# Gate products, residual and second normalisation on other engines in a fused Mamba and expert layer

## The chip, the core and the metric

The kernel runs on one core of a Trainium2 chip. The metric is device time in microseconds of one execution, median of several; inputs and outputs are float32 throughout.

## What is computed

For x of 4 batches of 2048 positions and 256 channels, with a modulation (sa, ca, ga, sb, cb, gb) computed from a small vector per batch:

```
h = layernorm(x) * (1 + ca) + sa
xs, res = split(h @ in_proj.T)
u = silu(conv4(xs) + conv_b)                    # 512 inner channels
dt, B, C = split(u @ x_proj.T)
delta = softplus(dt @ dt_proj.T + dt_b)
h_t = exp(delta*A) * h_{t-1} + (delta*u) * B    # 16 states per channel
y = sum_n(h_t * C) * silu(res)
x = x + ga * (y @ out_proj.T)
h = layernorm(x) * (1 + cb) + sb
x = x + gb * (shared expert(h) + best of 7 routed experts(h), by their gates)
```

An expert is `(silu(h @ w1b) * (h @ w1a)) @ w2`. The gate of the shared expert is a softmax over one logit.

## The kernel before

Two stages follow one another. The first, `fused_program`, takes all 8192 positions in 16 chunks of 512 (`NCHUNK`, `T`); it does everything up to the shared expert and writes rows and logits to memory. The second routes each position to one expert and runs the experts, tile by tile; the change does not touch it.

In a chunk the 512 channels times 16 states are cut into 16 sets of 32 channels (`NSET`); a set fills 128 partitions with 4 groups of states, so it has four scans of 128 x 512. For each set s of chunk c:

- SyncE spreads delta over the partitions by DMA (`spread_delta`), and ScalarE makes dA = exp(A * delta) into one of three PSUM banks (`exps`, L703, `ABANK`), so that it can be three scans ahead.
- The input delta*u*B of the set is written into one of eight state buffers `hs` (`RING`): for ten sets by VectorE, out of `u_ps` where TensorE spread delta*u (L816), for six sets (2, 5, 7, 10, 13, 15) by GpSimd, out of `u_rep`, spread by DMA (L986). GpSimd works in `states_in` only when the sum of the states that were in the buffer is made (`y_ready`).
- VectorE runs the four scans (L829). ScalarE saves the last column (L728), after which GpSimd multiplies the states by C (`weigh_states`, L993). TensorE adds up 16 states of four sets at a time: groups SUM 0 to 3 (L507), which VectorE gates with silu(res) (L838).

Everything else is woven between the scans. The work of a chunk is staggered: its front part (T, XS, CV, RS, XP, DT, DB: transposed normalised x, the projections, convolution, delta) runs one chunk ahead, its back part (OP: output projection; T2, RB, GL, B, A, Y: second normalised rows turned, written out, logits, shared expert) one chunk late. Four tables written out by hand say in which set each engine does what, with an offset that says for which chunk: `plan` for TensorE, `evict` for ScalarE (after which of the set's four exponentials), `vector` for VectorE (after which scan), `gps` for GpSimd, and `transfers` the order of SyncE's queue. Each engine and queue runs strictly in the order of its table.

TensorE's groups go to three banks: what ScalarE reads shares two, in the order of the plan; what VectorE reads (`VECTOR`, L225: SUM, OP, DB, A, Y) shares the third. A group waits until the group before it in its bank is read.

What the change and the prediction name:

- `weigh_u` (L800, at L804): delta*u for half a chunk, 128 x 1024, both inputs in SBUF, on VectorE; DU in the tables.
- `gate_norm` (L854 to L862): exp/sum for the shared gate, on VectorE: reciprocal, product, reciprocal, product, of 128 x 4.
- `residual` (L840, L845): x plus the output projection out of PSUM, on VectorE.
- `layernorm2` (L781 to L790): statistics of the second normalisation on VectorE; `rsqrt`, `rsqrt2` (L953 to L969): the inverse roots of both normalisations on GpSimd, by a power; `normalize`, `normalize2` (L650, L656) on ScalarE.
- `exp_table` (L647): loads ScalarE's table set that has both exponential and logarithm. SU is silu of u, SR and SS silu of res and of the shared expert's gate half, ET the loading of that set, E and L exponential and logarithm of the softplus.

## Time and profile before

| | |
|---|---|
| time, median of 3 runs | 2807.65 us (2804.6 to 2808.03) |
| the profiled execution | 2804.95 us, span 2803.1 us |
| busy: TensorE, VectorE, ScalarE, GpSimd | 2235.7, 2189.8, 1434.2, 1891.8 us |
| scan stage | from 76 us to 2226 us, first product with u_ps to last scan |
| expert stage | from 2300 us on |
| ScalarE table loads in four chunks | 28 (L648 8, L721 8, L633, L637, L641 4 each) |

A busy time counts an engine's instructions, without its waits. In a row of a group "busy, mean ns of one" is followed by the idle time of the engine just before those instructions and by what ended it. A float32 product of TensorE gives two records.

### The profile page before, as it was taken

The numbers are of one execution on the slowest core, as the hardware profiler recorded it, in microseconds if no ns is written. First come the engines' busy times: TensorE is split into PE (matmuls) and PEld (weight loads), VectorE is DVE, ScalarE is ACT, GpSimd is POOL, SyncE is SP. The second block draws the span as 40 slices with busy tenths as digits, with TensorE's granted clock in tenths as the row PEclk, the third lists the DMA queues.
The fourth block names the chain that finished last, engine by engine and source line by source line (L and its number), as shares of the span: only waits on it lengthen the run. The fifth ranks groups of instructions, "written<-read, shape, count | busy, mean of one in ns | idle before, by whom it ended". The sixth has DMA issues, their size and how long they took to land. (4 is left out here: it accounts for less than half of the span.)

```text
span 2803.1 us, 31106 instructions
## 1 busy us (share of the span) xinstructions
PE 2235.7 (80%) x7664; PEld 1062.5 (38%) x7665; DVE 2189.8 (78%) x2130; ACT 1434.2 (51%) x2391; POOL 1891.8 (67%) x800
## 2 busy tenths in 40 slices
PE   7759787978787788878786969697975656999997
PEld 3214332433333333434242424242432334666564
DVE  2799999998999999999999999999999625222222
ACT  4566474747474747474656565656554313222221
POOL 0788777777786878787868687777878602555553
PEclk9778999888889998989898989898986877999999
DMA  4433141313231323232323232323232124222221
GB/s 127 145 96 92 52 98 49 97 53 99 61 92 54 92 56 89 61 91 72 80 68 79 70 77 77 81 75 82 66 80 64 35 62 152 88 83 86 84 87 48
DMA packets 149399, 224.38 MB, mean 80 GB/s; under 512 B 48227, under 2 KB 85617, under 8 KB 145138
## 3 DMA queue, kind: packets, MB, share of 16 engines
q1 hardware_dynamic: 136914, 186.63, 25.3%
q0 software_dynamic: 12320, 35.93, 4.3%
q8 instruction: 57, 0.93, 0.2%
q14 instruction: 108, 0.88, 0.1%
HBM read 99.48 MB, written 31.47 MB: 47 GB/s over the span
## 5 line engine op out<-in xcount | busy, mean ns | idle before, releaser
L993 POOL TENSOR_TENSOR hs<-hs,c_rep 128x2048 f32<-128x2048 f32 x256 | 1170.2, 4585 | 258.1 <-ACT state L728 257.6
L721 ACT ACTIVATE dA<-d_rep,a 128x512 f32<-128x512 f32 x1024 | 689.9, 686 | 591.9 <-DVE hs L829 583.9
L829 DVE TENSOR_TENSOR_SCAN hs<-dA,state,hs 128x512 f32<-128x512 f32 x768 | 930.4, 1262 | 34.3 <-ACT dA L721 30.4
L986 POOL TENSOR_TENSOR hs<-u_rep,b_rep 128x2048 f32<-128x2048 f32 x96 | 444.9, 4634 | 181.1 <-DMA u_rep<-us 173.2
L478 PE MATMUL bank<-n,w1s 128*128 128x512 f32 x512 | 278.3, 676 | 142.9 <-DVE xpad L852 128.7
L816 DVE TENSOR_TENSOR hs<-u_ps,b_rep 128x2048 f32<-128x2048 f32 x160 | 361.4, 2276 | 9.8 <-PE u_ps L497 5.0
L507 PE MATMUL bank<-hs,spread 128*32 128x512 f32 x2048 | 297.0, 732 | 54.7 <-POOL hs L993 50.0
L436 PE MATMUL bank<-xin,w_in 128*128 128x512 f32 x512 | 268.9, 663 | 58.1 <-ACT xdbl L603 48.1
L829 DVE TENSOR_TENSOR_SCAN hs<-dA,hs 128x512 f32<-128x512 f32 x256 | 294.4, 1202 | 21.4 <-ACT dA L721 20.5
L1365 DVE TENSOR_TENSOR hid<-z,sg 128x512 f32<-128x512 f32 x70 | 48.4, 692 | 297.9 <-ACT sg L1343 297.9
L1283 PE MATMUL z<-w1r,hT 128*128 x560 | 260.8, 609 | 3.0 <-issue 2.0
L440 PE MATMUL bank<-xpad,w_conv 128*128 128x512 f32 x512 | 226.3, 595 | 0.0
L478 PEld LDWEIGHTS bank<-n,w1s 128*128 128x128 f32 x512 | 98.7, 209 | 297.6 <-DVE xpad L852 166.0
L497 PE MATMUL u_ps<-us,spread 32*128 32x512 f32 x320 | 189.5, 683 | 0.0
L455 PE MATMUL bank<-w_out,res 128*128 128x256 f32 x512 | 138.4, 432 | 49.3 <-DVE res L838 47.7
L436 PEld LDWEIGHTS bank<-xin,w_in 128*128 128x128 f32 x512 | 101.2, 206 | 201.5 <-issue 130.5
L507 PEld LDWEIGHTS bank<-hs,spread 128*32 128x32 f32 x2048 | 71.9, 131 | 273.8 <-issue 236.9
L1250 POOL DMA_INDIRECT out<-outr,cur x70 | 70.8, 1011 | 142.8 <-DVE outr L1358 140.4
L447 PE MATMUL bank<-xdbl,w_dt 65*128 65x512 f32 x256 | 137.1, 650 | 34.5 <-ACT n L614 14.7
L1283 PEld LDWEIGHTS z<-w1r,hT 128*128 128x128 f32 x560 | 101.4, 191 | 120.8 <-issue 120.6
L1343 ACT ACTIVATE sg<-z 128x512 f32<-128x512 f32 x70 | 41.8, 597 | 201.8 <-PE z L1283 196.2
L455 PEld LDWEIGHTS bank<-w_out,res 128*128 128x128 f32 x512 | 110.5, 218 | 87.7 <-issue 52.4
(174 smaller groups left out, 2718.9 us busy)
## 6 DMA issues: line engine op xcount, KB each, us to landing
d_rep<-delta SPq DMA_DIRECT2D x1024, 64.0 KB, 2.0
u_rep<-us SPq DMA_DIRECT2D x384, 64.0 KB, 2.0
b_rep<-bc_rows SPq DMA_DIRECT2D x64, 256.0 KB, 4.4
c_rep<-bc_rows SPq DMA_DIRECT2D x64, 256.0 KB, 7.4
xin<-in_x SPq DMA_DIRECT2D x16, 512.0 KB, 7.6
xres<-in_x SPq DMA_DIRECT2D x16, 512.0 KB, 3.6
token_rows<-xpad SPq DMA_DIRECT2D x32, 256.0 KB, 2.9
token_rows<-xres SPq DMA_DIRECT2D x16, 512.0 KB, 2.9
```

Of the source, the lines that this page charges most:

```text
L436: last = nc.tensor.matmul(ps_[:, :], t["w_in"][:, k, col:col + P], hT[:, k, :], start=(k == 0), stop=(k == KD - 1))
L440: last = nc.tensor.matmul(ps_[:, :], t["w_conv"][:, j, k, :], xpad[:, j, k:k + T], start=(k == 0), stop=(k == KCONV - 1))
L455: last = nc.tensor.matmul(ps_[:, h * D:(h + 1) * D], res[:, (par + off) % 2, k, tt * P:(tt + 1) * P], t["w_out"][:, k, :], start=(k == 0), ...
L478: last = nc.tensor.matmul(ps_[:, :], t["w1s"][:, k, col:col + P], h2T[:, k, :], start=(k == 0), stop=(k == KD - 1))
L497: nc.tensor.matmul(u_ps[:, i % 2, :], t["spread"][DS * q:DS * q + DS].rearrange("p f d -> p (f d)"), us[DS * q:DS * q + DS, par, j, :], st ...
L507: last = nc.tensor.matmul(ps_[DS * q:DS * q + DS, :], t["gather"], hs[:, (SPC * j + q) % RING, n, :], start=(n == 0), stop=(n == NG - 1), ...
L721: nc.scalar.activation(dA[:, u % ABANK, :], d_rep[:, q, :], ACT.Exp, scale=t["a"][:, u:u + 1]).then_inc(da_ready, 1)
L816: nc.vector.tensor_tensor(hs[:, s % RING], u_ps[:, i % 2, :].unsqueeze(1).to_broadcast([P, NG, T]), b_rep[:, par, :].rearrange("p (g t) -> ...
L829: nc.vector.tensor_tensor_scan(hs[:, s % RING, g, :], dA[:, u % ABANK, :], hs[:, s % RING, g, :], state[:, u:u + 1] if m else 0.0, ALU.mul ...
L986: nc.gpsimd.tensor_tensor(hs[:, s % RING], u_rep[:, i % UBUF, :].unsqueeze(1).to_broadcast([P, NG, T]), b_rep[:, par, :].rearrange("p (g t ...
L993: nc.gpsimd.tensor_tensor(hs[:, s % RING, :, :], hs[:, s % RING, :, :], c_rep[:, par, :].rearrange("p (g t) -> p g t", g=NG), ALU.mult).th ...
L1283: last = nc.tensor.matmul(z[:, q % 2, half, :], hT[:, q % 2, i, :], t["w1r"][:, e, i, half * H:(half + 1) * H], start=(i == 0), stop=(i == ...
```

## The change

GpSimd makes delta*u (`weigh_u`) in place of VectorE, except for chunk 0. The gate's two products become eight copies with a scale on ScalarE (`gate_times`: GM0, GM1), VectorE keeps the two reciprocals (RC). The residual is added by TensorE, as a product of xres with the identity in the group OP; ScalarE reads OP out of PSUM and sums the rows as it does so. The second normalisation is wholly on ScalarE: mean and squares (N2A, with sums accumulated), inverse root as exp(-0.5 ln) (N2B), the rows in two halves (N2C0, N2C1); the inverse root of the first normalisation goes there too (NA), and its rows are normalised in halves (NC0, NC1). `mhalf` and GpSimd's root functions go. SU is now silu followed by `exp_table`; SRS is silu of res of the next chunk, silu of the shared expert's half of the chunk before, and `exp_table`. OP moves from VectorE's bank to ScalarE's two. All five tables are arranged anew. At the start of the kernel c and x are loaded before A, and delta*u of chunk 0 stays on VectorE (`weigh_first_u`).

```diff
-            1: [(('XS', 2), 1), (('DB', 3), 0), (('XS', 3), 1), (('SUM', 3), -1)],
-            2: [(('CV', 0), 1), (('CV', 1), 1), (('OP', 0), -1)],
+            1: [(('XS', 2), 1), (('DB', 3), 0), (('XS', 3), 1), (('CV', 0), 1), (('SUM', 3), -1), (('CV', 1), 1), (('OP', 0), -1)],
+            2: [],
             3: [(('CV', 2), 1), (('CV', 3), 1), (('OP', 1), -1)],
-            4: [],
-            5: [(('SUM', 0), 0), (('RS', 0), 1), (('RS', 1), 1)],
-            6: [(('XP', 0), 1), (('RS', 2), 1)],
-            7: [(('RS', 3), 1), (('T2', 0), -1), (('T2', 1), -1)],
-            8: [(('DT', 0), 1), (('DT', 1), 1), (('RB', 0), -1), (('RB', 1), -1)],
-            9: [(('SUM', 1), 0), (('GL', 0), -1), (('B', 0), -1), (('B', 1), -1)],
-            10: [(('DB', 0), 1), (('B', 2), -1), (('B', 3), -1)],
-            11: [(('DT', 2), 1), (('DB', 1), 1), (('DT', 3), 1)],
-            12: [(('A', 0), -1), (('T', 0), 2)],
-            13: [(('SUM', 2), 0)],
-            14: [(('T', 1), 2), (('A', 1), -1), (('A', 2), -1), (('A', 3), -1), (('Y', 0), -1)],
-            15: []}
+            4: [(('SUM', 0), 0)],
+            5: [(('RS', 0), 1), (('RS', 1), 1)],
+            6: [],
+            7: [(('XP', 0), 1), (('RS', 2), 1), (('RS', 3), 1), (('T2', 0), -1), (('T2', 1), -1)],
+            8: [(('DT', 0), 1), (('RB', 0), -1), (('DT', 1), 1)],
+            9: [(('B', 0), -1), (('SUM', 1), 0), (('RB', 1), -1), (('GL', 0), -1), (('B', 1), -1)],
+            10: [(('B', 2), -1), (('B', 3), -1), (('DB', 0), 1)],
+            11: [(('DT', 2), 1), (('DB', 1), 1), (('A', 0), -1), (('DT', 3), 1)],
+            12: [],
+            13: [(('SUM', 2), 0), (('T', 0), 2)],
+            14: [(('A', 1), -1), (('A', 2), -1), (('T', 1), 2), (('A', 3), -1)],
+            15: [(('Y', 0), -1)]}
...
+            0: [[], [], [(('XS', 0), 1)], [(('XS', 1), 1)]],
+            1: [[], [(('XS', 2), 1), (('XS', 3), 1)], [], [(('CV', 0), 1)]],
+            2: [[], [], [(('CV', 1), 1)], []],
+            3: [[], [], [], []],
+            4: [[(('OP', 0), -1), (('CV', 2), 1)], [(('CV', 3), 1)], [(('HALO', 0), 2)], []],
+            5: [[(('OP', 1), -1), (('N2A', 0), -1)], [(('N2B', 0), -1)], [], []],
+            6: [[(('N2C1', 0), -1), (('SU', 0), 1)], [(('N2C0', 0), -1)], [], [(('RS', 0), 1), (('RS', 1), 1)]],
+            7: [[], [], [], []],
+            8: [[(('XP', 0), 1)], [(('RS', 2), 1), (('RS', 3), 1)], [(('T2', 0), -1), (('T2', 1), -1), (('DT', 0), 1)], [(('DT', 1), 1), (('RB', 0), -1)]],
+            9: [[], [], [], [(('E0', 0), 1)]],
+            10: [[], [(('RB', 1), -1), (('L0', 0), 1), (('B', 0), -1)], [], []],
+            11: [[(('GL', 0), -1)], [], [(('B', 1), -1)], []],
+            12: [[(('B', 2), -1), (('B', 3), -1), (('SRS', 0), 0), (('G', 0), -1)], [], [], []],
+            13: [[(('NA', 0), 2), (('DT', 2), 1), (('NC1', 0), 2), (('NC0', 0), 2)], [], [(('DT', 3), 1), (('E1', 0), 1)], []],
+            14: [[(('GM0', 0), -1)], [], [], []],
+            15: [[(('GM1', 0), -1), (('L1', 0), 1)], [], [(('T', 0), 2), (('T', 1), 2)], []]}
...
             0: [[(('Y', 1), -2)], [], [(('DB', 2), 0)], []],
-            1: [[(('DB', 3), 0), (('DU', 1), 0)], [], [], []],
-            2: [[], [], [(('SUM', 3), -1)], []],
-            3: [[], [], [], [(('OP', 0), -1)]],
-            4: [[], [], [], [(('OP', 1), -1)]],
+            1: [[(('DB', 3), 0)], [], [], [(('SUM', 3), -1)]],
+            2: [[], [], [], []],
+            3: [[], [], [], []],
+            4: [[], [], [], []],
             5: [[], [], [], []],
-            6: [[(('LN2', 0), -1)], [], [(('SUM', 0), 0)], []],
+            6: [[(('SUM', 0), 0)], [], [], []],
             7: [[], [], [], []],
             8: [[], [], [], []],
             9: [[], [], [], []],
             10: [[(('SUM', 1), 0)], [], [], []],
-            11: [[(('LN', 0), 2)], [(('DB', 0), 1)], [], [(('DB', 1), 1)]],
-            12: [[(('DU', 0), 1)], [], [], [(('A', 0), -1)]],
-            13: [[], [], [], [(('SUM', 2), 0), (('G1', 0), -1)]],
-            14: [[(('A', 1), -1)], [], [(('A', 2), -1)], []],
+            11: [[], [(('LN', 0), 2), (('DB', 0), 1)], [], [(('DB', 1), 1)]],
+            12: [[], [], [], [(('A', 0), -1)]],
+            13: [[], [(('RC', 0), -1)], [], [(('SUM', 2), 0)]],
+            14: [[], [(('A', 1), -1), (('RC', 1), -1)], [(('A', 2), -1)], []],
             15: [[(('A', 3), -1)], [], [], [(('Y', 0), -1)]]}
         gps = {
-            0: [(('IN', 5), 0)],
+            0: [(('DU', 1), 0), (('IN', 5), 0), (('IN', 7), 0)],
             1: [],
             2: [],
-            3: [(('IN', 7), 0)],
-            4: [(('R2', 0), -1), (('IN', 10), 0)],
+            3: [],
+            4: [],
             5: [],
             6: [],
-            7: [],
+            7: [(('IN', 10), 0)],
             8: [],
             9: [],
-            10: [(('G0', 0), -1), (('R', 0), 2), (('IN', 13), 0)],
-            11: [],
-            12: [(('IN', 15), 0)],
-            13: [(('IN', 2), 1)],
+            10: [(('G0', 0), -1), (('IN', 13), 0)],
+            11: [(('DU', 0), 1), (('IN', 15), 0)],
+            12: [],
+            13: [],
             14: [],
-            15: []}
-        transfers = [('U', 5), ('ACC2', 0), ('XR', 0), ('D', 4), ('D', 5), ('W2', 0), ('D', 6), ('U', 7), ('D', 8), ('WO', 0), ('D', 7), ('U', 10),
-                     ('D', 9), ('D', 10), ('D', 11), ('BC', 0), ('U', 13), ('X', 0), ('D', 12), ('ROWS', 0), ('D', 13), ('LOG', 0), ('U', 15), ('D', 14),
-                     ('D', 15), ('D1', 2), ('D1', 0), ('U1', 2), ('D1', 1), ('D1', 3)]
+            15: [(('IN', 2), 1)]}
+        transfers = [('U', 5), ('ACC2', 0), ('XR', 0), ('D', 4), ('U', 7), ('D', 5), ('D', 6), ('D', 8), ('WO', 0), ('D', 7), ('W2', 0), ('U', 10),
+                     ('D', 9), ('D', 10), ('D', 11), ('BC', 0), ('U', 13), ('X', 0), ('D', 12), ('ROWS', 0), ('D', 14), ('D', 15), ('D', 13), ('U', 15),
+                     ('LOG', 0), ('D1', 2), ('D1', 0), ('U1', 2), ('D1', 3), ('D1', 1)]
...
-        VECTOR = ("SUM", "OP", "DB", "A", "Y")
+        VECTOR = ("SUM", "DB", "A", "Y")
...
+                        pe.wait_ge(xres_loaded, 16 * f + 16)
                     for h in range(2):
+                        tt = 2 * j + h
+                        nc.tensor.matmul(ps_[:, h * D:(h + 1) * D], t["ident"][:], xres[:, tt, :], start=True, stop=False)
                         for k in range(KI):
-                            tt = 2 * j + h
                             last = nc.tensor.matmul(ps_[:, h * D:(h + 1) * D], res[:, (par + off) % 2, k, tt * P:(tt + 1) * P], t["w_out"][:, k, :],
-                                                    start=(k == 0), stop=(k == KI - 1))
+                                                    start=False, stop=(k == KI - 1))
...
+                elif kind == "OP":
+                    for h in range(2):
+                        tt = 2 * j + h
+                        last = nc.scalar.activation(xres[:, tt, :], ps_[:, h * D:(h + 1) * D], ACT.Copy, accum_out=sum2[:, tt:tt + 1])
+                    last.then_inc(x1_ready, 1)
...
-            def normalize(f):
-                act.wait_ge(shift_ready, f + 1)
+            def inverse_root(rstd_, shift_, mean_, var_, scale, done, n):
+
+                nc.scalar.activation(rstd_[:], var_, ACT.Ln, scale=scale, bias=eps[:, 0:1]).then_inc(done, 1)
+                act.wait_ge(done, n + 1)
+                nc.scalar.activation(rstd_[:], rstd_[:], ACT.Exp, scale=-0.5).then_inc(done, 1)
+                act.wait_ge(done, n + 2)
                 for tt in range(TT):
+                    last = nc.scalar.activation(shift_[:, tt:tt + 1], mean_[:, tt:tt + 1], ACT.Copy, scale=rstd_[:, tt:tt + 1])
+                last.then_inc(done, 1)
+                act.wait_ge(done, n + 3)
...
+            def statistics(f):
+                act.wait_ge(stats_ready, f + 1)
+                nc.scalar.activation(mv[:, :, 0], mv[:, :, 0], ACT.Copy, scale=-1.0).then_inc(small, 1)
+                act.wait_ge(small, 4 * f + 1)
+                inverse_root(rstd, shift, mv[:, :, 0], mv[:, :, 1], 1.0, small, 4 * f + 1)
...
+                act.wait_ge(x1_ready, 2 * f + 2)
+                nc.scalar.activation(mean2[:], sum2[:], ACT.Copy, scale=-1.0 / D).then_inc(small2, 1)
+                act.wait_ge(small2, 4 * f + 1)
                 if not (known(f) and f == 0):
                     act.wait_ge(a_made, KI * f)
                 for tt in range(TT):
+                    last = nc.scalar.activation(n2[:, tt, :], xres[:, tt, :], ACT.Square, bias=mean2[:, tt:tt + 1], accum_out=sum2[:, tt:tt + 1])
+                last.then_inc(squares, 1)
+
+            def statistics2(f):
+                act.wait_ge(squares, f + 1)
+                inverse_root(rstd2, shift2, mean2, sum2[:], 1.0 / D, small2, 4 * f + 1)
...
+            def gate_times(f, i):
+
+                act.wait_ge(gate_inv, 2 * f + i + 1)
+                for tt in range(TT):
+                    last = nc.scalar.activation(gs[:, 1, tt:tt + 1], gs[:, 0, tt:tt + 1], ACT.Copy, scale=gs[:, 1, tt:tt + 1])
+                last.then_inc(gate_soft if i == 0 else gate_ready, 1)
...
                 if kind == "SU":
                     silu_u(f, half)
-                elif kind == "SR":
-                    silu_res(f, half)
-                elif kind == "SS":
-                    silu_shared(f)
-                elif kind == "ET":
                     exp_table()
...
+                if g[0] == "SRS":
+                    if not (known(c) and c + 1 >= NCHUNK):
+                        silu_res(c + 1, (m + 1) % 2)
+                    if not (known(c) and c == 0):
+                        silu_shared(c - 1)
+                    exp_table()
...
-            def layernorm2(f):
-                hold(dve, x1_ready, 2 * f + 2, held)
...
-                hold(dve, ln2_step, f + 1, held)
...
-                last.then_inc(stats2_ready, 1)
...
-            def weigh_u(f, half, h):
-                dve.wait_ge(delta_ready, KI * f + 2 * h + 2)
-                dve.wait_ge(us_ready, f + 1)
-                dve.wait_ge(xdbl_made, f + 1)
-                nc.vector.tensor_tensor(us[:, half, 2 * h:2 * h + 2], delta[:, 2 * h:2 * h + 2], us[:, half, 2 * h:2 * h + 2], ALU.mult).then_inc(du_ready, 1)
...
-            def residual(f, j):
-
...
-                nc.vector.tensor_tensor(xres[:, 2 * j:2 * j + 2, :], ps_[:].rearrange("p (h d) -> p h d", h=2), xres[:, 2 * j:2 * j + 2, :],
-                                        ALU.add).then_inc(x1_ready, 1)
...
-            def gate_norm(f):
-                dve.wait_ge(gate_exp, f + 1)
-                nc.vector.reciprocal(gs[:, 0, :], gs[:, 1, :]).then_inc(gate_step, 1)
-                dve.wait_ge(gate_step, 3 * f + 1)
-                nc.vector.tensor_tensor(gs[:, 0, :], gs[:, 1, :], gs[:, 0, :], ALU.mult).then_inc(gate_step, 1)
-                dve.wait_ge(gate_step, 3 * f + 2)
-                nc.vector.reciprocal(gs[:, 1, :], gs[:, 0, :]).then_inc(gate_step, 1)
-                dve.wait_ge(gate_step, 3 * f + 3)
-                nc.vector.tensor_tensor(gs[:, 1, :], gs[:, 0, :], gs[:, 1, :], ALU.mult).then_inc(gate_ready, 1)
+            def gate_inverse(f, i):
+                if i == 0:
+                    dve.wait_ge(gate_exp, f + 1)
+                else:
+                    dve.wait_ge(gate_soft, f + 1)
+                nc.vector.reciprocal(gs[:, 0, :], gs[:, 1, :]).then_inc(gate_inv, 1)
...
-            def rsqrt(f):
-                hold(pool, stats_ready, f + 1, held)
-                nc.gpsimd.tensor_scalar(mv[:, :, 1], mv[:, :, 1], EPS, None, ALU.add).then_inc(rstd_step, 1)
...
-                nc.gpsimd.tensor_tensor(rstd[:], mv[:, :, 1], t["mhalf"][:, 0:TT], ALU.pow).then_inc(rstd_step, 1)
...
+            def weigh_u(f, half, h):
+                hold(pool, delta_ready, KI * f + 2 * h + 2, held)
+                pool.wait_ge(us_ready, f + 1)
+                pool.wait_ge(xdbl_made, f + 1)
+                nc.gpsimd.tensor_tensor(us[:, half, 2 * h:2 * h + 2], delta[:, 2 * h:2 * h + 2], us[:, half, 2 * h:2 * h + 2], ALU.mult).then_inc(du_ready, 1)
```

## Rows read from the trace of the kernel before

**Rows 1.** The page: busy time of each engine, and VectorE's slices

```profile
PE 2235.7 (80%) x7664; PEld 1062.5 (38%) x7665; DVE 2189.8 (78%) x2130; ACT 1434.2 (51%) x2391; POOL 1891.8 (67%) x800
...
DVE  2799999998999999999999999999999625222222
```

**Rows 2.** Timeline of VectorE, L784: start, length; its first and fifteenth

```profile
243.84 1.38 DVE L784 BATCH_NORM_STATS2 stats<-xres 128x6 f32<-128x256 f32 x4
...
2146.97 1.38 DVE L784 BATCH_NORM_STATS2 stats<-xres 128x6 f32<-128x256 f32 x4
```

**Rows 3.** Four periods: length, busy (instructions) by engine, clock, DMA

```profile
925.45:1469.57 544.12, 435.46 (x1485) 191.65 (x1486) 508.65 (x456) 324.72 (x526) 415.81 (x125) 0.90 0.30 76
```

**Rows 4.** Groups of VectorE in those periods: busy, mean ns, idle before

```profile
L829 DVE TENSOR_TENSOR_SCAN hs<-dA,state,hs 128x512 f32<-128x512 f32 x192 | 232.8, 1262 | 8.1 <-ACT dA L721 7.0 <-DVE hs L816 1.1
...
L829 DVE TENSOR_TENSOR_SCAN hs<-dA,hs 128x512 f32<-128x512 f32 x64 | 73.8, 1202 | 2.8 <-ACT dA L721 2.5
L804 DVE TENSOR_TENSOR us<-delta,us 128x1024 f32<-128x1024 f32 x8 | 36.9, 4614 | 0.1
L862 DVE TENSOR_TENSOR gs<-gs 128x4 f32<-128x4 f32 x4 | 16.8, 4204 | 0.1
L858 DVE TENSOR_TENSOR gs<-gs 128x4 f32<-128x4 f32 x4 | 13.2, 3302 | 0.1
...
L784 DVE BATCH_NORM_STATS2 stats<-xres 128x6 f32<-128x256 f32 x16 | 5.5, 408 | 0.0
L845 DVE TENSOR_TENSOR xres<-bank,xres 128x512 f32<-128x512 f32 x8 | 5.5, 684 | 7.0 <-PE bank L455 7.0
...
L790 DVE BATCH_NORM_AGGREGATE mv<-stats 128x2 f32<-128x6 f32 x16 | 1.5, 157 | 1.1 <-DVE stats L784 1.1
```

**Rows 5.** Single lines: ns at least, median, at most

```profile
L829 DVE TENSOR_TENSOR_SCAN hs<-dA,state,hs x768: 1249/1258/1285, 195.9 to 2224.8; 128x512 f32<-128x512 f32 x192
...
L804 DVE TENSOR_TENSOR us<-delta,us x32: 1224/3842/5599, 66.9 to 2109.6; 128x1024 f32<-128x1024 f32 x32
...
L858 DVE TENSOR_TENSOR gs<-gs x16: 164/3208/3576, 304.7 to 2278.5; 128x4 f32<-128x4 f32 x16
...
L993 POOL TENSOR_TENSOR hs<-hs,c_rep x256: 4486/4527/5537, 94.3 to 2226.5; 128x2048 f32<-128x2048 f32 x128
```

**Rows 6.** Groups of GpSimd in the four periods

```profile
L993 POOL TENSOR_TENSOR hs<-hs,c_rep 128x2048 f32<-128x2048 f32 x65 | 297.4, 4588 | 67.9 <-ACT state L728 67.9
L986 POOL TENSOR_TENSOR hs<-u_rep,b_rep 128x2048 f32<-128x2048 f32 x24 | 111.8, 4659 | 48.0 <-DMA u_rep<-us 47.1 <-PE bank L507 0.6
L967 POOL TENSOR_TENSOR rstd<-mv,mhalf 128x4 f32<-128x4 f32 x4 | 4.2, 1038 | 0.7 <-POOL mv L965 0.7
```

**Rows 7.** Groups of ScalarE in the four periods

```profile
L728 ACT ACTIVATE state<-hs 128x4 f32<-128x4 f32 x64 | 12.5, 196 | 0.0
...
L721 ACT ACT_TABLE_LOAD x8 | 10.3, 1283 | 0.1
...
L661 ACT ACTIVATE n<-xres,shift,rstd 128x256 f32<-128x256 f32 x16 | 8.3, 589 | 2.1 <-POOL shift L969 2.1
...
L633 ACT ACT_TABLE_LOAD x4 | 5.1, 1283 | 0.1
```

**Rows 8.** Group of ScalarE, whole span

```profile
L1326 ACT ACTIVATE hT<-t_ps 128x256 f32<-128x256 f32 x70 | 26.4, 378 | 14.2 <-PE t_ps L1273 14.2
```

**Rows 9.** Timeline of VectorE: start, length, instructions

```profile
940.58 9.50 DVE L829 TENSOR_TENSOR_SCAN hs<-dA,state,hs 128x512 f32<-128x512 f32 x8
...
1008.18 4.48 DVE L816 TENSOR_TENSOR hs<-u_ps,b_rep 128x2048 f32<-128x2048 f32 x2
```

**Rows 10.** Timeline of TensorE: start, length, instructions

```profile
1021.82 3.64 PE L507 MATMUL bank<-hs,spread 128*32 128x512 f32 x32
...
1041.84 7.03 PE L440 MATMUL bank<-xpad,w_conv 128*128 128x512 f32 x16
```

**Rows 11.** Group of TensorE in the four periods

```profile
L455 PE MATMUL bank<-w_out,res 128*128 128x256 f32 x128 | 34.4, 430 | 11.8 <-DVE res L838 11.8
```

129 lines of the change are left out of this document (51 added, 78 removed).

## The prediction

> **What bounds the kernel now.** I read the page's first parts, then a period, then the groups within it. The page gives VectorE (DVE) 78% of the span, but its slices show 9 tenths from the third to the thirty-first and 2 to 6 after: the share averages the scan stage and the later expert stage, which the change does not touch [rows 1]. The period of the scan stage comes from an operation that occurs once a chunk: between its occurrences at 243.84 and 2146.97 us lie 14 chunks, so 1903.13 / 14 = 135.9 us each [rows 2]. In four periods in the middle VectorE is busy 508.65 of 544.12 us, that is 127.2 of 136.0 a chunk; TensorE has 108.9, GpSimd 104.0, ScalarE 81.2 [rows 3]. So VectorE bounds, with 8.9 us of waits a chunk, and what is taken from it is worth its time until the next engine is full.
>
> Its groups [rows 4] tell two kinds of work apart. The product delta*u (L804) takes 4.61 us for 1024 elements, though its shortest is 1.22 us; the gate products (L858, L862) take 3.3 and 4.2 us for four elements, the shortest 0.16 us, which is the last, after the scans [rows 4, 5]. Both inputs of all three lie in SBUF. A scan reads PSUM and SBUF and varies by no more than 36 ns [rows 5]. So it is these products, not VectorE as such, that wait while GpSimd works. The Trainium skill says so too: in "SBUF — State Buffer", section "Who interferes with whom", a VectorE instruction with two SBUF inputs contends with a GpSimd one that reads SBUF. By that rule nothing left in the loop after the change would contend; the trace agrees.
>
> **What leaves VectorE, per chunk** (each group of [rows 4] divided by its four chunks). delta*u: 36.9 / 4 = 9.2 us. Gate products: (16.8 + 13.2) / 4 = 7.5. The second normalisation's statistics (L784, L790): (5.5 + 1.5) / 4 = 1.8, and 0.3 of waiting for its own result. Residual (L845): 5.5 / 4 = 1.4, and 7.0 / 4 = 1.8 of waiting for the bank. The two reciprocals stay. That is 22.0; neighbouring records overlap by some 0.07 us (8 scans in 9.50 us, against 1.26 each [rows 9]) and about a dozen go, so I take off 0.9: **21.1 us, which leaves 114.8 a chunk** if every other wait stays as it is.
>
> **Where it goes.** GpSimd: its product of 2048 elements takes 4.49 us at the shortest [rows 5], 4.59 on average [rows 6]. No row has 1024 elements there: a half, 2.25, is one bound, the full 4.5 the other. I take 2.3, since the four-element products of this engine are far below (even the power, L967, takes 1.04) and the rate decides. Two are 4.6. The small operations of both inverse roots leave, at least 2 x 1.04 and three of 0.2 with each: 3.4. The large products lose what VectorE's reads stretched, at most 0.1 x 22 = 2.2; I take 2.0. So 104.0 + 4.6 - 3.4 - 2.0 = 103.2 of 114.8, and today's wait for u_rep, 47.1 / 4 = 11.8 a chunk [rows 6], is slack. The moved product waits for delta and for u, ahead of all that the in-order queue holds: behind delta*u(1) stand the inputs of sets 5 and 7, then the weighing of sets 1 and on. VectorE needs set 5 some 25 us later, which is the cover; I cost this at nothing, and if the cover goes it is rival D. On SyncE's queue the transfer of u for set 7 moves ahead of two of delta, and that of delta for set 13 behind two: at nothing as well, as each still has a set of 7 us before its reader; a late one would hold ScalarE's exponentials, and all behind them.
>
> The Trainium skill speaks against the move: "GPSIMD Engine Reference", section "Engine selection", wants elementwise products on VectorE and calls GpSimd about twice as slow with two inputs. By that alone a chunk would pay 2 x 2.4 for 2 x 1.2 us, and the first term would be 2.4 in place of 9.2. The row of 4.61 us differs, and it decides.
>
> ScalarE, a chunk: the residual out of PSUM, four 128x256 with an accumulated sum, between 0.38 (a plain copy out of PSUM [rows 8]) and 0.59 (SBUF, with scale and bias [rows 7]); I take 0.5, so 2.0. Four squares at 0.52: 2.1. Two inverse roots with their means: 14 tiny operations at 0.2 (as L728 [rows 7]) 2.8. Gate products, eight tiny ones: 1.6. Together 8.5. An accumulator's read-out, which no row shows, could add 0 to 0.25 to each of eight, at most 2. Against it: today seven table loads a chunk of 1.28 us. The load ahead of the silu of u is thrown away by that silu, and the set that the next exponential then picks has no logarithm, so there is a pair of loads round the logarithm (two at L721 and one at L633 a chunk [rows 7]). After the change each silu is followed by the set with both, four loads, so 3 x 1.28 = 3.8 leave. ScalarE gets 81.2 + 4.7 = 86 of 115: not the bound by its total, but it keeps only three exponentials ahead, 3 x 1.19 = 3.6 us of scans, and a longer block stops the scan.
>
> TensorE: 16 products with w_out take 34.4 / 4 = 8.6 us, 0.54 each [rows 11]; four more for the residual are 2.2. So 111 of 115 busy, at a granted clock of 0.90 [rows 3]. Part of that length is half clock: a group of the convolution takes 3.5 us at full clock (two in 7.03, 32 records as 16 here [rows 10]), and the mean of its engine is longer. With the waits behind the gate products gone it should be granted more; I take 105 to 111.
>
> **New waits.** (1) SUM 3 is now made behind CV 0, and used at the end of set 1, not in set 2. A chunk begins with the product at 1008.18 [rows 9]; TensorE ended SUM 3 at 1021.82 + 3.64 = 1025.46, 17.3 us in [rows 10]; with 3.5 in front it is 20.8. VectorE gets there after 4.48 for two products [rows 9], 8 scans of 1.19, 0.8 for Y and 2 x 0.6 for DB: 16 us in. So it waits up to 4.8; as a wait of VectorE lets the others run ahead, I take half, 2.4. (2) ScalarE's blocks. Half of the second normalisation (1.0), then silu of u between two table loads, 1.28 + 1.9 + 1.28, with 0.6 for the next exponential: 6.1 us; VectorE has three scans and one 0.6, 4.2: 1.9 over. Residual and squares (3.3) and the root (1.2) in set 5, with one scan's work between: 1.4 over. Together 3.3. (3) Given back: of the (7.0 + 2.5) / 4 = 2.4 us that scans wait for dA today [rows 4] I put most, 2.0, down to the loads round the logarithm. Sum 2.4 + 3.3 - 2.0 = 3.7, so **118.5 us a chunk**.
>
> **The total.** All of it applies in 15 chunks. Chunk 0 has no gate, residual or statistics of a chunk before, and one moved product: 3 us. The end of the stage is a chain without cover: squares and roots on ScalarE against 1.8 on VectorE and 2 on GpSimd now, and the gate's hand-overs, some 3 us more. At the start ScalarE's roots stand in for GpSimd's: 0. So 15 x (135.9 - 118.5) + 3 - 3 = 261. The profiled execution took 2804.95 us (span 2803.1), 2.7 below the median of 2807.65: 2804.95 - 261 = 2544, and at the median's offset 2546.
>
> **Bounds.** Low: the 21.1 and the 2.0 given back, no new wait: 112.8, so 15 x 23.1 = 347, and 2458. High: no relief on either wait (4.8 + 3.3), 2 us of read-outs in ScalarE's blocks, nothing given back: 124.9, so 165, and 2640.
>
> **Rivals.**
> A, the removed time is all there is: 112.8 to 116 a chunk, 2458 to 2505; at 114.8, 2804.95 - 15 x 21.1 = 2488. For it: the tables of all engines move together, and the first normalisation's statistics now stand opposite ScalarE's long silu block. Against: the count under (1). Chance 0.30.
> B, TensorE and ScalarE in turn become the bound: TensorE stays at 111 us busy, and 30 of its groups instead of 28 wait for ScalarE to free one of two banks: 122 to 125 a chunk, about 2625. For: 111 of 115 is 97%. Against: it idles 27 us a chunk today, and its slow stretches stand behind those idles. Chance 0.17.
> C, the chain from SUM 3 through residual, squares, root, transposition, B, A to Y no longer fits one chunk and stretches it to 130: 2804.95 - 15 x 5.9 = 2716. Chance 0.04.
> D, slower: GpSimd's queue. delta*u(1) and the inputs of sets 5 and 7 stand ahead of the weighing of sets 1 to 3 and each waits for another party (delta; SUM 3; the transfer for set 7, behind a store and a load of xres). The weighing frees the ring of eight state buffers. It decides once these waits pass 136 - 103 = 33 us a chunk; at 35 the period is 138 and the time 2804.95 + 15 x 2.1 = 2836. Against: SUM 3 comes 21 us in, where GpSimd would otherwise be some 18 us in, and it gains 1 to 2 us a set afterwards. Chance 0.03.
> That the change doesn't do what it says has one form here, an accumulated sum that runs as two instructions; it is in the high bound.
>
> **Chances.** Forecast (117 to 121.5 a chunk, 2505 to 2590) 0.46, A 0.30, B 0.17, C 0.04, D 0.03. The range leaves out C, D and the outer edges of A and B: 2468 to 2620. A measurement of this kernel can tell about 0.2%, 6 us. Faster by more than that 0.97, within it 0.01, slower 0.02.
>
> **What would show it.** Right: a period near 118.5; no two-input SBUF product on VectorE in the loop; delta*u at 2.3 us on GpSimd; four table loads a chunk; a wait of 2 to 5 us for SUM 3 and one of about 2 before the scans of set 6; a granted clock above 0.90. Wrong: delta*u over 3 us on GpSimd; scans longer than 1.26; GpSimd idle under 3 us a chunk, which would make it the bound; or VectorE idle above 15 us a chunk over many banks, which is rival B.

## The result, and the profile after

The changed kernel takes 2703.4 us in the median of four runs (2687.4 to 2714.2), the kernel before beside it 2807.8 (2804.6 to 2810.3): a ratio of 0.962, with a 95% interval of 0.958 to 0.967. The gain is 104 us where 261 were forecast, and the time lies above the range. Its profiled execution took 2703.2 us with a span of 2701.1.

The page, with VectorE's slices and TensorE's granted clock:

```profile
PE 2281.9 (84%) x7792; PEld 1087.0 (40%) x7793; DVE 1902.9 (70%) x1908; ACT 1502.6 (56%) x2955; POOL 1880.1 (70%) x702
...
DVE  2798888887888798888878888888889343222222
...
PEclk9779898898988898989898989898977778999999
```

VectorE lost 287 us of busy time [rows 1], more than the kernel gained: it did get rid of its work, and then waited. Its slices say so, mostly 8 where there was a 9. TensorE leads now, by far.

The period, by the first statistics of a chunk in VectorE's timeline (an operation that both kernels have):

```profile
278.72 1.38 DVE L828 BATCH_NORM_STATS2 stats<-xin 128x6 f32<-128x256 f32 x4
...
1834.26 1.38 DVE L828 BATCH_NORM_STATS2 stats<-xin 128x6 f32<-128x256 f32 x4
```

Twelve chunks lie between: 1555.54 / 12 = 129.6 us, where 118.5 were forecast. Before it was 135.9 by the operation of [rows 2], of whose 14 intervals the last is a short one (2016.94 to 2146.97 us, 130.0); by this operation (L772 there, at 278.81 and 1916.28 us) it was 136.5, so the change brings 6.9 us a chunk. Four periods, in the columns of [rows 3]:

```profile
929.80:1449.71 519.91, 449.41 (x1522) 198.51 (x1520) 433.75 (x401) 341.91 (x668) 414.29 (x101) 0.89 0.32 80
```

Of 130.0 us a chunk VectorE is busy 108.4 and idle 21.5, where it was idle 8.9. GpSimd has 103.6 (forecast 103.2) and ScalarE 85.5 (forecast 86). TensorE has 112.4 at a clock of 0.89, not 105 to 111 above 0.90. So every engine's work is about what was forecast, and nearly all that is missing is waiting. Where VectorE waits, in the same four periods by groups:

```profile
L873 DVE TENSOR_TENSOR_SCAN hs<-dA,state,hs 128x512 f32<-128x512 f32 x193 | 234.2, 1265 | 20.7 <-ACT dA L771 19.1 <-DVE hs L860 1.6
L860 DVE TENSOR_TENSOR hs<-u_ps,b_rep 128x2048 f32<-128x2048 f32 x40 | 90.4, 2278 | 8.8 <-PE u_ps L499 6.5 <-issue 2.3
L873 DVE TENSOR_TENSOR_SCAN hs<-dA,hs 128x512 f32<-128x512 f32 x64 | 74.1, 1206 | 8.6 <-ACT dA L771 8.3
L841 DVE SCALAR_TENSOR_TENSOR delta<-bank,delta 128x512 f32<-128x512 f32 x16 | 10.9, 679 | 27.1 <-PE bank L447 27.1
...
L882 DVE TENSOR_TENSOR res<-bank,res 128x512 f32<-128x512 f32 x16 | 10.8, 674 | 14.4 <-PE bank L509 14.4
```

The scans are as long as before, 1265 and 1206 ns for 1262 and 1202 [rows 4]. DB (L841), the first half of delta, is what a reader should stop at: 16 small operations wait 27.1 us, 6.8 a chunk, and the forecast had no wait there. A stretch of VectorE's timeline has the three waits of a chunk that matter:

```profile
929.80 1.38 DVE L828 BATCH_NORM_STATS2 stats<-xin 128x6 f32<-128x256 f32 x4
931.53 0.38 DVE L834 BATCH_NORM_AGGREGATE mv<-stats 128x2 f32<-128x6 f32 x4 [0.35 <-DVE stats L828]
...
940.61 0.69 DVE L841 SCALAR_TENSOR_TENSOR delta<-bank,delta 128x512 f32<-128x512 f32 x1 [8.70 <-PE bank L447]
...
993.67 0.69 DVE L882 TENSOR_TENSOR res<-bank,res 128x512 f32<-128x512 f32 x1 [3.36 <-PE bank L509]
...
1027.53 1.28 DVE L873 TENSOR_TENSOR_SCAN hs<-dA,state,hs 128x512 f32<-128x512 f32 x1 [3.35 <-ACT dA L771]
```

DB 0 waits 8.70 us at once, SUM 3 3.36, and the scan behind ScalarE's block of set 6 3.35. The last two are the waits that the forecast named. What comes ahead of DB in TensorE's timeline:

```profile
1030.44 5.37 PE L444 MATMUL bank<-us,w_x 128*97 128x512 f32 x8 [2.91 <-ACT res L594]
...
1045.79 1.98 PE L480 MATMUL bank<-n,w1s 128*128 128x512 f32 x4
1048.27 3.64 PE L509 MATMUL bank<-hs,spread 128*32 128x512 f32 x32 [0.50 <-POOL hs L1008]
1051.84 0.66 PE L469 MATMUL bank<-ident,n 128*128 128x128 f32 x4
1054.62 3.31 PE L474 MATMUL bank<-wg,n 128*128 128x8 f32 x16 [2.12 <-ACT xpad L632]
1057.78 3.76 PE L480 MATMUL bank<-n,w1s 128*128 128x512 f32 x4
```

GL (L474) waits 2.12 us for L632, by which ScalarE reads B 0 out of the bank that GL needs. Only after it come B 1 (the L480 row), B 2, B 3 and then DB 0. The L480 row ahead of SUM 1 (L509) is B 0 itself.

The moved work on ScalarE and GpSimd, first ScalarE's groups in the four periods:

```profile
L655 ACT ACT_TABLE_LOAD x8 | 10.3, 1283 | 0.1
...
L686 ACT ACTIVATE n<-xres,mean 128x256 f32<-128x256 f32 x16 | 7.9, 496 | 0.1
...
L706 ACT ACTIVATE gs<-gs 128x1 f32<-128x1 f32 x32 | 6.8, 282 | 0.4 <-DVE gs L895 0.4
L616 ACT ACTIVATE xres<-bank 128x256 f32<-128x256 f32 x16 | 5.9, 373 | 6.5 <-PE bank L457 6.5
...
L616 ACT ACTIVATION_READ_ACCUMULATOR xres<-bank 128x1 f32 x16 | 3.1, 197 | 0.0
...
L686 ACT ACTIVATION_READ_ACCUMULATOR n<-xres,mean 128x1 f32 x16 | 3.0, 186 | 0.0
```

and GpSimd's group of the moved product in the same stretch:

```profile
L984 POOL TENSOR_TENSOR us<-delta,us 128x1024 f32<-128x1024 f32 x8 | 18.9, 2365 | 0.0
```

2.37 us for delta*u was 2.3 in the forecast; the squares take 0.50 (0.52), the residual copy 0.37 (0.5). An accumulator's read-out is an instruction of its own of 0.19 to 0.20. A gate copy takes 0.28, not 0.2.

### The profile page after: what moved, and what is told of

The parts are those of the page before. It is cut to its first block and busy times, and to the rows that moved or that the text cites. A ratio compares the mean times of both kernels' runs of the same rounds, so it can differ in the third digit from the quotient of the medians.

```text
span 2701.1 us, 31467 instructions
## 1 busy us (share of the span) xinstructions
PE 2281.9 (84%) x7792; PEld 1087.0 (40%) x7793; DVE 1902.9 (70%) x1908; ACT 1502.6 (56%) x2955; POOL 1880.1 (70%) x702
## 5 line engine op out<-in xcount | busy, mean ns | idle before, releaser
L1008 POOL TENSOR_TENSOR hs<-hs,c_rep 128x2048 f32<-128x2048 f32 x256 | 1154.4, 4523 | 378.1 <-ACT state L778 378.0
L873 DVE TENSOR_TENSOR_SCAN hs<-dA,state,hs 128x512 f32<-128x512 f32 x768 | 931.0, 1265 | 78.7 <-ACT dA L771 73.7
L1001 POOL TENSOR_TENSOR hs<-u_rep,b_rep 128x2048 f32<-128x2048 f32 x96 | 434.7, 4535 | 86.8 <-DMA u_rep<-us 86.4
L509 PE MATMUL bank<-hs,spread 128*32 128x512 f32 x2048 | 295.0, 728 | 127.3 <-POOL hs L1008 125.6
L480 PE MATMUL bank<-n,w1s 128*128 128x512 f32 x512 | 315.0, 754 | 54.9 <-DVE delta L841 25.1
L873 DVE TENSOR_TENSOR_SCAN hs<-dA,hs 128x512 f32<-128x512 f32 x256 | 295.0, 1205 | 34.8 <-ACT dA L771 33.9
L436 PE MATMUL bank<-xin,w_in 128*128 128x512 f32 x512 | 247.0, 622 | 8.2 <-ACT xin L585 8.2
L509 PEld LDWEIGHTS bank<-hs,spread 128*32 128x32 f32 x2048 | 71.6, 130 | 352.6 <-issue 246.8
L480 PEld LDWEIGHTS bank<-n,w1s 128*128 128x128 f32 x512 | 107.9, 230 | 227.3 <-issue 111.5
L447 PE MATMUL bank<-xdbl,w_dt 65*128 65x512 f32 x256 | 148.0, 674 | 40.2 <-ACT n L621 14.7
L440 PEld LDWEIGHTS bank<-xpad,w_conv 128*128 128x128 f32 x512 | 94.4, 189 | 133.3 <-issue 130.9
L488 PE MATMUL bank<-w2s,xpad 128*128 128x256 f32 x512 | 118.7, 385 | 17.6 <-DVE xres L903 15.8
(171 smaller groups left out, 2636.3 us busy)
```

Source lines behind the costliest of these rows:

```text
L436: last = nc.tensor.matmul(ps_[:, :], t["w_in"][:, k, col:col + P], hT[:, k, :], start=(k == 0), stop=(k == KD - 1))
L440: last = nc.tensor.matmul(ps_[:, :], t["w_conv"][:, j, k, :], xpad[:, j, k:k + T], start=(k == 0), stop=(k == KCONV - 1))
L447: last = nc.tensor.matmul(ps_[:, :], t["w_dt"][:, j * P:(j + 1) * P], xdbl[0:DT_ROWS, :], start=True, stop=True)
L480: last = nc.tensor.matmul(ps_[:, :], t["w1s"][:, k, col:col + P], h2T[:, k, :], start=(k == 0), stop=(k == KD - 1))
L509: last = nc.tensor.matmul(ps_[DS * q:DS * q + DS, :], t["gather"], hs[:, (SPC * j + q) % RING, n, :], start=(n == 0), stop=(n == NG - 1), ...
L873: nc.vector.tensor_tensor_scan(hs[:, s % RING, g, :], dA[:, u % ABANK, :], hs[:, s % RING, g, :], state[:, u:u + 1] if m else 0.0, ALU.mul ...
```

## The experiments

The theory at the outset: the parts bring what was forecast, and the new order of the tables makes TensorE late for DB. The rivals: a part brings less than its busy time; the moved table loads cost; TensorE is simply full.

**The two moves alone.** The first kernel is the one before with the gate products on ScalarE:

```diff
-            13: [[], [], [], [(('SUM', 2), 0), (('G1', 0), -1)]],
-            14: [[(('A', 1), -1)], [], [(('A', 2), -1)], []],
+            13: [[], [(('RC', 0), -1)], [], [(('SUM', 2), 0)]],
+            14: [[(('A', 1), -1)], [(('RC', 1), -1)], [(('A', 2), -1)], []],
...
+            14: [[(('GM0', 0), -1)], [], [], []],
+            15: [[(('GM1', 0), -1), (('L1', 0), 1)], [(('T', 0), 2)], [(('T', 1), 2)], []]}
```

> The kernel before with one part of the change: the gate's two products on ScalarE (eight small copies), the two reciprocals stay on VectorE; every table else as before. VectorE loses 7.5 us of 127 a chunk. Theory T (TensorE's in-order work, 112 us busy with its half-clock stretches and some 18 us of waits, holds the changed kernel at 130 us a chunk): here there are 136 us, so most of the 7.5 is still gained, 5 to 7.5 a chunk, 2700 to 2735 us. Theory S (ScalarE's long blocks starve the scans): ScalarE gets 2.5 us more in pieces under 1 us, no loss: the same. If instead the period of 130 is set by the order of the new tables alone (theory O), the full 7.5 comes, 2697.

It took 2677.2 us, ratio 0.953 (0.951 to 0.955), less than any of the times expected. The second has delta*u on GpSimd alone:

```diff
-            1: [[(('DB', 3), 0), (('DU', 1), 0)], [], [], []],
+            1: [[(('DB', 3), 0)], [], [], []],
...
-            12: [[(('DU', 0), 1)], [], [], [(('A', 0), -1)]],
+            12: [[], [], [], [(('A', 0), -1)]],
...
+            0: [(('DU', 1), 0), (('IN', 5), 0)],
...
+            11: [(('DU', 0), 1)],
```

> The kernel before with one other part: delta*u on GpSimd (set 11 and set 0 of its table), all else as before. VectorE loses 9.2 us a chunk, GpSimd gets 4.7. Theory T: 5 to 9 us a chunk, 2670 to 2730. Theory O: the full 9.2, about 2670. If the queue of GpSimd were to hold (its wait for delta ahead of the input of set 5), less than 4 us a chunk, over 2745.

It took 2698.6 us, 0.962 (0.960 to 0.964), inside the wider of the expected ranges and short of the full 9.2 us. The third has the edits of both:

> The kernel before with both parts, gate products on ScalarE and delta*u on GpSimd, in the old tables; residual and second normalisation stay on VectorE. VectorE's work falls to 110.5 us a chunk. If VectorE still bounded with its old waits: 136 - 16.7 = 119 a chunk, 2555 us. Theory T: TensorE has 109 us of work and its waits, so the period can't fall much under 127: 2650 to 2690. Theory O: 119 to 122, 2555 to 2600.

It took 2611.2 us, 0.930 (0.929 to 0.932), between the times of theory O and theory T. So each move is worth its busy time or near it: the gate 130 us, 8.7 for each of 15 chunks against 7.5 of products, delta*u 109 or 7.2 against 9.2. By the first statistics of a chunk, over the same twelve chunks as above, the period fell by 8.0 us with the gate's move (136.5 to 128.5) and by 7.9 with delta*u's (to 128.6), so the two are nearly alike within the loop. Together they gain 196 of the 238 that the two add up to. These two parts of the change alone beat the whole change by 92 us: that much is lost in the rest of the change.

**Is TensorE full?** The changed kernel with one of the convolution's four products (this leaves out three of the four taps):

```diff
-                    for k in range(KCONV):
+                    for k in range(1):
```

> The changed kernel with three of the convolution's four products left out in the scan stage (TensorE computes one tap), so TensorE has 10.6 us less a chunk and nothing else changes. Theory T: the period falls by 6 to 11 us, to 119 to 124, about 2540 to 2610 us, and VectorE's waits for banks shrink. Theory S: ScalarE's work is the same, the period falls by less than 2 us, over 2670.

2636.3 us, 0.939 (0.938 to 0.941): 67 us less than the change, 4.5 a chunk for some 10.5 of TensorE's (three quarters of four groups of 3.5 us [rows 10]). That lies between the two theories' times and bears out neither. The granted clock fell to 0.865, and VectorE still waited for DB, 5.7 us a chunk, in 600 us of this kernel:

```profile
L841 DVE SCALAR_TENSOR_TENSOR delta<-bank,delta 128x512 f32<-128x512 f32 x18 | 12.2, 679 | 27.4 <-PE bank L447 27.4
```

So TensorE's work ahead of the stretch is not the main reason that DB is late. What shrank in those 600 us were the scans' waits for dA, from 28.3 to 14.1; why was not tried.

**The table loads.** The kernel with both moves and the loading of the set behind the silu of u, so four loads a chunk for seven:

```diff
-            5: [[], [(('CV', 3), 1), (('HALO', 0), 2), (('ET', 0), 1)], [(('SU', 0), 1)], []],
+            5: [[], [(('CV', 3), 1), (('HALO', 0), 2)], [(('SU', 0), 1), (('ET', 0), 1)], []],
```

> The two parts in the old tables (run before, 2611 us), with the combined table set loaded behind the silu of u instead of two scans ahead of it, as the change does: four loads a chunk for seven, 3.8 us of ScalarE less. Theory S (ScalarE's blocks hold the scans, which wait 4.8 us a chunk for dA in the run with both parts): 2 to 4 us a chunk, 2550 to 2580. Theory T (TensorE's order and clock): under 1 us a chunk, over 2595.

2615.8 us, 0.932 (0.931 to 0.934), 5 more than without. Three loads less a chunk, 3.8 us of ScalarE, bring nothing, and the scans' waits for dA in 600 us are 21.9 for 21.8: the loads did not hold them.

**Parts or order.** Two kernels cross them. The first has all parts of the change in the order of the tables before, with the moved operations put near their predecessors' places (of its edit, two sets of ScalarE's table):

```diff
-            5: [[(('OP', 1), -1), (('N2A', 0), -1)], [(('N2B', 0), -1)], [], []],
+            5: [[], [(('CV', 3), 1), (('HALO', 0), 2)], [(('SU', 0), 1), (('OP', 1), -1)], []],
+            6: [[(('N2A', 0), -1), (('RS', 0), 1), (('RS', 1), 1)], [(('N2B', 0), -1)], [], []],
```

> Every part of the change, in the tables of before with the moved operations put near their old places (ScalarE reads OP 0 at the end of set 3 and OP 1 in set 5, squares at the start of set 6, root one exponential later, rows in set 7). Theory O (the new order of the tables costs, not the parts): VectorE has 5 us less work than in the run with both parts, 2530 to 2600. Theory M (moving the residual to TensorE and the second normalisation to ScalarE costs: 2 us more on TensorE, 9 on ScalarE, and OP in ScalarE's two banks, where every later group waits for it): 2640 to 2710.

2625.6 us, 0.935 (0.934 to 0.937), at a clock of 0.91, between the two theories' times. The other has the two moves alone, in the order of the change's tables (of its edit, three lines of TensorE's and ScalarE's tables):

```diff
-            9: [(('SUM', 1), 0), (('GL', 0), -1), (('B', 0), -1), (('B', 1), -1)],
+            9: [(('B', 0), -1), (('SUM', 1), 0), (('RB', 1), -1), (('GL', 0), -1), (('B', 1), -1)],
...
-            10: [(('DB', 0), 1), (('B', 2), -1), (('B', 3), -1)],
+            10: [(('B', 2), -1), (('B', 3), -1), (('DB', 0), 1)],
...
-            10: [[(('L0', 0), 1), (('RB', 1), -1)], [], [(('B', 0), -1), (('GL', 0), -1)], []],
+            10: [[], [(('RB', 1), -1), (('L0', 0), 1), (('B', 0), -1)], [], []],
```

> The changed kernel's order of the tables, with only the two parts in it: residual and the second normalisation's statistics on VectorE, roots on GpSimd, as before. Theory O: as slow as the changed kernel or nearly, 2670 to 2730, with VectorE waiting for DB 0 behind B 2 and B 3. Theory M: near the run with both parts in the old tables, 2590 to 2630.

2697.9 us, 0.961 (0.960 to 0.963), as theory O had it. The same parts are 78 us faster in the old order, and the two moves 87 us slower in the new one: **most of the loss is the order's.** The groups of DB in 600 us, in the kernel of the old order

```profile
L841 DVE SCALAR_TENSOR_TENSOR delta<-bank,delta 128x512 f32<-128x512 f32 x20 | 13.5, 677 | 3.2 <-PE bank L447 3.1
```

and in that of the new

```profile
L805 DVE SCALAR_TENSOR_TENSOR delta<-bank,delta 128x512 f32<-128x512 f32 x20 | 13.5, 677 | 33.2 <-PE bank L447 33.2
```

show that the wait goes with the order. In the old one the residual and the second normalisation bring no more: 2625.6 is 14 above the 2611.2 of the two moves alone. There the parts do cost waits. The scans of the two moves alone, in 600 us,

```profile
L837 DVE TENSOR_TENSOR_SCAN hs<-dA,state,hs 128x512 f32<-128x512 f32 x248 | 300.5, 1263 | 18.1 <-ACT dA L729 16.4 <-DVE hs L824 1.7
...
L837 DVE TENSOR_TENSOR_SCAN hs<-dA,hs 128x512 f32<-128x512 f32 x64 | 74.0, 1204 | 5.7 <-ACT dA L729 5.4
```

wait 16.4 + 5.4 = 21.8 us for dA; with all parts in the old order it is 34.8, and the waits for u_ps are 19.5 us for 1.8.

**Which entry.** The change also moved DB 0 behind B 2 and B 3 in set 10, and that was my first guess. This kernel is the change with the old order of the three:

```diff
-            10: [(('B', 2), -1), (('B', 3), -1), (('DB', 0), 1)],
+            10: [(('DB', 0), 1), (('B', 2), -1), (('B', 3), -1)],
```

> The changed kernel with one line moved: TensorE makes DB 0 ahead of B 2 and B 3 in set 10, not behind them. VectorE waits 6.8 us a chunk for DB 0 in the changed kernel. Theory O: that wait is the order's, it falls by 3.7 us (two groups) or more, and the period by 3 to 6: 2610 to 2655. Theory T (TensorE is behind as a whole, so the wait reappears at B's readers on ScalarE and at dA): less than 2 us a chunk, over 2675.

The guess was wrong: 2746.9 us, 0.978 (0.977 to 0.980), some 44 more than the change. The waits moved, as theory T had it: VectorE's timeline has DB 0 2.13 us late, where the stretch above had 8.70, and DB 1 now 4.13:

```profile
1351.04 0.69 DVE L841 SCALAR_TENSOR_TENSOR delta<-bank,delta 128x512 f32<-128x512 f32 x1 [2.13 <-PE bank L447]
1351.65 2.45 DVE L873 TENSOR_TENSOR_SCAN hs<-dA,state,hs 128x512 f32<-128x512 f32 x2
...
1358.23 0.69 DVE L841 SCALAR_TENSOR_TENSOR delta<-bank,delta 128x512 f32<-128x512 f32 x1 [4.13 <-PE bank L447]
```

B 2 was now what came late. ScalarE waited 5.62 us for it, ahead of its long silu block, and the scans' waits for dA in 600 us rose from 28.3 to 42.7. Later TensorE's SUM 2 waited for the weighed states:

```profile
1369.73 6.50 PE L509 MATMUL bank<-hs,spread 128*32 128x512 f32 x32 [6.86 <-POOL hs L1008]
```

Both orders leave TensorE late in this stretch, so what makes it late stands before. Three kernels then each remove one of the waits that precede it. GpSimd's input of set 7 is put back behind the weighing (ahead of SUM 0, which waits 2.63 us):

```diff
-            0: [(('DU', 1), 0), (('IN', 5), 0), (('IN', 7), 0)],
+            0: [(('DU', 1), 0), (('IN', 5), 0)],
...
-            3: [],
+            3: [(('IN', 7), 0)],
```

> The changed kernel with one entry of GpSimd's table put back: the input of set 7 behind the weighing of set 3, not ahead of the weighing of set 1. TensorE waits 2.6 us a chunk for that weighing ahead of SUM 0, and then sums at half clock, 5.2 us for 3.6. Theory W (three waits of TensorE, each followed by work at half clock, make it late for DB 0): the wait goes, 2 to 4 us a chunk, 2640 to 2675. Rival V (VectorE's and ScalarE's own order is what costs, TensorE's waits are filled later anyway): under 1 us a chunk, over 2688.

2697.3 us, 0.962 (0.960 to 0.964): 6 less than the change, inside the spread of its runs. TensorE's waits in 600 us of this kernel:

```profile
PE bank L444 <- ACT res L594: 24.6, 4, 6.2
PE bank L509 <- POOL hs L1008: 20.8, 13, 4.8
```

In the change the two are 13.1 and 28.8: what went ahead of the sums came back ahead of XP. Next ScalarE reads RS 0 and 1 sooner, for which XP waits 2.91 us:

```diff
-            6: [[(('N2C1', 0), -1), (('SU', 0), 1)], [(('N2C0', 0), -1)], [], [(('RS', 0), 1), (('RS', 1), 1)]],
+            6: [[(('N2C1', 0), -1), (('SU', 0), 1)], [(('RS', 0), 1), (('RS', 1), 1), (('N2C0', 0), -1)], [], []],
```

> The changed kernel with RS 0 and RS 1 read by ScalarE at the second exponential of set 6 instead of the fourth. TensorE waits 2.9 us a chunk for their banks ahead of XP, and then takes 5.4 to 6.5 us for XP's 3.6. Theory W: 2 to 4 us a chunk, 2640 to 2675. Rival V: over 2688.

2700.1 us, 0.962 (0.961 to 0.964): nothing. TensorE's waits in 600 us of this kernel show why:

```profile
PE bank L509 <- POOL hs L1008: 25.3, 12, 3.0
PE bank L436 <- ACT xdbl L605: 11.8, 5, 2.8
```

The wait for RS (13.1 us in the change) has gone and one for xdbl has come, a group or two later. Last, ScalarE reads B 0 a set earlier, ahead of an exponential instead of behind RB 1 and a logarithm:

```diff
-            9: [[], [], [], [(('E0', 0), 1)]],
-            10: [[], [(('RB', 1), -1), (('L0', 0), 1), (('B', 0), -1)], [], []],
+            9: [[], [], [], [(('B', 0), -1), (('E0', 0), 1)]],
+            10: [[], [(('RB', 1), -1), (('L0', 0), 1)], [], []],
```

> The changed kernel with B 0 read by ScalarE at the end of set 9 instead of in set 10. TensorE waits 2.1 us a chunk for its bank ahead of GL, and then takes 3.3 and 3.8 us for GL's 1.95 and B 1's 1.9, all directly ahead of DB 0. Theory W: 3 to 5 us a chunk, 2625 to 2660, and VectorE's wait of 6.8 us for DB 0 falls by as much. Rival V: over 2688.

**2607.4 us, 0.929 (0.928 to 0.930): one entry of a table gives 96 us,** 6.4 a chunk and more than the 3 to 5 expected. TensorE's timeline in this kernel:

```profile
987.64 3.67 PE L444 MATMUL bank<-us,w_x 128*97 128x512 f32 x8 [2.73 <-ACT res L594]
...
1002.20 3.78 PE L480 MATMUL bank<-n,w1s 128*128 128x512 f32 x4
1005.91 3.98 PE L509 MATMUL bank<-hs,spread 128*32 128x512 f32 x32
1009.82 0.66 PE L469 MATMUL bank<-ident,n 128*128 128x128 f32 x4
1010.31 1.85 PE L474 MATMUL bank<-wg,n 128*128 128x8 f32 x16
1012.02 1.96 PE L480 MATMUL bank<-n,w1s 128*128 128x512 f32 x4
```

The wait of XP for RS stands as it did. GL follows RB 1 at once and takes 1.85 us for 3.31, B 1 takes 1.96 for 3.76. So it is in nearly all chunks, not only in this one; GL's single products over the whole run, for the change and for this kernel (ns at least, median, at most):

```profile
L474 PE MATMUL bank<-wg,n x256: 256/361/379, 272.4 to 2164.1; 128*128 128x8 f32 x128
...
L474 PE MATMUL bank<-wg,n x256: 175/256/382, 269.6 to 2069.6; 128*128 128x8 f32 x128
```

In the change GL waits for the read of B 0 in all 16 chunks, 32.0 us in all, and here in none. Here the granted clock is 1.00, in the change 0.52; the windows of GL and B 1, and below them of XP, are for the change

```profile
1054.62:1061.54 6.92, 6.92 (x21) 4.38 (x21) 6.92 (x8) 3.33 (x7) 6.92 (x2) 0.52 0.33 99
1030.44:1035.81 5.37, 5.37 (x9) 2.07 (x10) 5.37 (x5) 3.67 (x7) 5.37 (x2) 0.68 0.30 73
```

and for this kernel

```profile
1010.31:1013.91 3.60, 3.60 (x22) 2.36 (x20) 3.34 (x5) 3.40 (x7) 3.40 (x2) 1.00 0.43 145
987.64:991.31 3.67, 3.67 (x9) 1.57 (x10) 3.67 (x4) 3.13 (x7) 3.67 (x2) 1.00 0.29 71
```

In the change the granted clock was still 1.00 from 1049.00 to 1054.00 us. So the read of B 0 costs 2.12 us of waiting and 3.3 of half clock (0.52 of full speed is the level of 1.2 GHz), 5.4 us at the place where VectorE waits for what follows. The Trainium skill describes the second half: "TensorE: Matmul & The Clock Gate", section "HAM oscillation — how this bites in real kernels", tells of a loop whose stalls bring the clock down again and again. The rows agree at GL. At XP they do not follow from the wait alone: it ran at full speed after 2.73 us, and here it is B 0, some 15 us later, that takes 3.78 us for 1.98. The half clock has not left this chunk, it lies ahead of GL and no longer on it. VectorE's groups, in 600 us of this kernel:

```profile
L841 DVE SCALAR_TENSOR_TENSOR delta<-bank,delta 128x512 f32<-128x512 f32 x19 | 12.9, 676 | 3.0 <-PE bank L447 2.8
...
L882 DVE TENSOR_TENSOR res<-bank,res 128x512 f32<-128x512 f32 x19 | 12.8, 673 | 17.9 <-PE bank L509 17.7
```

DB waits 3.0 us, which is 0.6 a chunk for 6.8. And four of its periods, but for the last 0.7 us (the fourth ends at 1513.68):

```profile
1017.39:1513.00 495.61, 435.14 (x1520) 191.29 (x1520) 433.04 (x401) 341.01 (x668) 413.45 (x101) 0.92 0.34 84
```

(1513.68 - 1017.39) / 4 = 124.1 us a chunk, with VectorE busy 108.4 as in the change and idle 15.6 for 21.5.

What do residual and second normalisation then bring, with the order mended? 4 us beside the two moves alone. VectorE has less work but waits more. 600 us of the kernel with the two moves:

```profile
900.00:1500.00 600.00, 520.60 (x1805) 229.10 (x1808) 541.41 (x531) 400.37 (x684) 525.00 (x160) 0.90 0.33 83
```

It is idle 9.8% there; in the stretch above (495.61 - 433.04) / 495.61 = 12.6%. What it gained in work it pays in waits: in 600 us 32.2 for dA against 21.8, 17.7 for SUM against 6.2 and 8.2 for u_ps against 1.8. The two kernels differ in their order as well. For dA and u_ps the kernels in the old order show the same with the parts alone; for SUM they hardly do (7.7 for 6.2), and with the two moves alone in the new order it is 14.3, so that wait belongs to the new order.

All three entries at once:

> The three edits together. Theory W: 7 to 11 us a chunk, 2540 to 2600, with VectorE's waits for DB 0 near 0 and a granted clock over 0.92. Rival V: over 2670.

2606.2 us, 0.929 (0.927 to 0.931): as with B 0 alone, and just above the 2540 to 2600 expected. These two are the fastest kernels here, and beat both the kernel before (by 201 us) and the change (by 97).

## Why the prediction was wrong

**Right: what leaves and where it goes.** VectorE's busy time fell by 127.2 - 108.4 = 18.8 us a chunk; of the 21.1 forecast 19.0 were busy time and the rest waiting. The totals of GpSimd and ScalarE came out within 0.5 us, and delta*u at 2.37. The reason given, products with both inputs in SBUF beside a working GpSimd, fits the two moves alone, though no run parts it from the products themselves: eight copies of 0.28 us in place of two products of 3.3 and 4.2 gained 130 us. The Trainium skill's page "SBUF — State Buffer", section "Who interferes with whom", agrees with this. Its page "GPSIMD Engine Reference", section "Engine selection", is right on the rate, 2.37 us on GpSimd against VectorE's shortest of 1.22 [rows 5], and not in its advice here, for 109 us were gained by the opposite.

**Wrong: the sum under "New waits".** It came to 3.7 us a chunk. From VectorE's groups in four periods of each kernel (before, in the same view as [rows 4], DB waited 1.5 us, SUM 2.0, u_ps 1.4 and A 5.9; dA 9.5) the waits grew, a chunk, by

| wait of VectorE for | forecast | the change | B 0 read early |
|---|---|---|---|
| DB | 0 | 6.4 | 0.3 |
| SUM | 2.4 | 3.1 | 3.1 |
| dA | 3.3 - 2.0 = 1.3 | 4.5 | 4.3 |
| u_ps | 0 | 1.3 | 1.3 |
| A | 0 | -0.6 | -0.2 |
| sum | 3.7 | 14.7 | 8.8 |

The 11.0 us between 3.7 and 14.7 are the 11.5 between 118.5 and 130.0 but for half a us. More than half is DB, and dA has 3.2. So the step that failed is this sum, which put the wait for DB at nothing. It had counted TensorE's way through the table for one stretch, from SUM 3's new place to the vector entry that uses it, and took the other stretches as they were. But B 0 now stands ahead of SUM 1, and RB 1 behind it, while ScalarE still reads B 0 behind RB 1. So TensorE's GL must wait for a read that must wait for TensorE's own RB 1 and a logarithm, and DB 0, now behind B 3, comes after all of it. Both tables stood in the diff; the trace of before had no such wait. That this read is the cause of the wait for DB is shown: it is the only entry changed in the kernel of 2607.4 us. It accounts for 96 of the 157 us between the forecast of 2546 and the measured 2703; the other 61 go with the waits for dA, SUM and u_ps that are left, which no run here removes.

**Wrong in size: what is given back.** 2.0 of the 2.4 us of waits for dA were to go with three table loads. They did not go: the kernel without those loads gained nothing, and the waits for dA grew by 4.5, not 1.3. About half of the growth is there with the two moves alone, whose ScalarE has only the gate's copies more: 4.5 us a chunk for 2.4 before. A VectorE with less work of its own meets the same blocks sooner, which the forecast had left out; that this is the reason is argued, not shown. The residual and the second normalisation bring about the other half. The wait behind set 6 is 3.35 us, where the forecast had 1.9; how the rest divides among the blocks was not tried.

**A slip in the bounds.** 117 us a chunk, the forecast's lower edge, is 2804.95 - 15 x 18.9 = 2521 us, not 2505; that is the time of rival A's 116. The measured time lies far above either.

**Rival B, in part.** VectorE does idle above 15 us a chunk, and 130 is longer than that rival's 125. And what it named, groups of TensorE that wait for ScalarE to free one of two banks, is what happened at GL. But not because TensorE was full: one entry of a table removes it, and 10.5 us less work on TensorE gave 4.5 a chunk and left most of DB's wait. Rival C, the chain from SUM 3 to Y, gave 2716 us, near the time measured, but by luck, for its mechanism is not the one found: VectorE's wait for its last link, Y, was 1.3 us in four chunks before and 1.5 after. Rival A's time is what VectorE's work would allow, and no kernel came near it. D did not come: GpSimd idles 26 us a chunk.

The ends of the stage were put at nothing. By the last scan, at 2224.8 us before [rows 5] and 2116.8 after, the scan stage gained 108 us; 2703.2 - 2116.8 = 586.4 against 2804.95 - 2224.8 = 580.2 is 6 us lost behind it, where 3 were forecast.

## What to carry to other kernels

When hand-written orders are moved, walk every in-order engine through the whole loop, and at each shared buffer ask of its reader: does it stand behind something that the waiting engine has yet to make? Where a change brings less than the busy time it takes away, run its parts in the old order and the old parts in the new one; that parts the order from the work. And of waits on an engine that does not bound, mend those between it and the first thing that the bounding engine waits for: of three waits of 2 to 3 us here, one was worth 96 us, and two next to nothing, as they came back a group or two later.

## What was not expected of the hardware

The four-element gate products cost a little more than their own length: the period fell by 8.0 us for 7.5 us of products, although the tables kept their order, and the rest of the 130 us came outside the twelve chunks measured; why was not tried. Waits of about the same length have different ends: XP takes 5.37 us after 2.91 us of waiting in the stretch of the change above, at a granted clock of 0.68 in this window, and 3.67 us after 2.73 where B 0 is read early, at 1.00. The kernel is not what parts the two, for both lengths occur in both: XP at 899.46 us of the change takes 3.67 after 2.90, and at 1234.05 where B 0 is read early 5.37 after 2.75. In both kernels B 0 takes 3.78 us in these chunks with the short XP and 1.98 in those with the long one. What decides between them was not found. And less work on TensorE lowered its clock: with one tap it was 0.865, for 0.887, which fits with the small gain.
